# Transposing transfers from SP in place of TensorE's turns of the q and k halves, in a language-model tower block

## The reference

```python
xn = layernorm(layernorm(h)) * norm_g + norm_b
q = heads(xn @ Wq);  k, v = heads(x @ Wkv)           # x = layernorm(h)
k, v = two learned null keys and values, then k, v   # 2050 keys
q = q / |q| * q_scale;  k = k / |k| * k_scale
sim = q @ k.T * 8 - slope(head) * distance           # causal
out = softmax(sim) @ v;  h = h + out @ Wout
```

## Time and profile before

| | |
|---|---|
| median of 3 runs | 2745.8 us (2736.39 to 2750.08) |
| profiled execution | 2751.77 us, span 2750.0 us |
| PE busy | 2424.1 us, 88% |
| DVE busy | 2027.2 us, 74% |
| POOL busy | 1594.1 us, 58% |
| ACT busy | 1406.6 us, 51% |
| mean granted PE clock | 0.948 of full |
| transfers | 106.65 MB, mean 39 GB/s |

### The profile page before, as it was taken

The page is one execution under the profiler, slowest core; times in us unless marked ns, Lnnn a source line. Parts: engine busy times, 40 slices in busy tenths (PEclk is TensorE's granted clock), DMA queues, the critical chain, the costliest instruction groups (busy, mean ns, idle before and its releaser), DMA issues.

```text
span 2750.0 us, 49117 instructions
## 1 busy us (share of the span) xinstructions
PE 2424.1 (88%) x13353; PEld 1204.6 (44%) x13353; DVE 2027.2 (74%) x5748; ACT 1406.6 (51%) x3094; POOL 1594.1 (58%) x1901
## 2 busy tenths in 40 slices
PE   2789999999989988898999999999999997877887
PEld 2434344444434434343444444444434443446775
DVE  6678787878777878878787878787878786644444
ACT  3445455655554646565555555554646563324541
POOL 6365656666675656575757575656565665462424
PEclk8899999999999999999999999999999998868999
DMA  2000111011111011011111000001000002023543
GB/s 46 18 19 19 34 25 37 24 36 26 30 45 23 24 25 31 20 34 28 34 28 30 17 22 15 25 16 25 16 25 15 21 15 82 9 86 112 163 128 123
DMA packets 155702, 106.65 MB, mean 39 GB/s; under 512 B 63728, under 2 KB 139632, under 8 KB 155440
## 3 DMA queue, kind: packets, MB, share of 16 engines
q1 hardware_dynamic: 147760, 82.52, 11.6%
q0 software_dynamic: 7680, 20.98, 2.5%
HBM read 52.94 MB, written 33.29 MB: 31 GB/s over the span
## 4 chain that ended last, share of the span: by engine, by line
PE 29%; DVE 10%; DMA 6%; issue 5%; POOL 2%; SPq 2%; ACT 2%; another core or an unknown queue 1%; ACTq 0%; DVEq 0%; POOLq 0%
PE ps L1474 5%; PE ps L1458 3%; DVE ps L1123 3%; PE ps L1459 3%; DMA rl<-l_row 3%; PE ps L1555 2%; PE ps L1431 2%; PE ps L1541 2%; PE ps L1403 2%; DMA l_row<-l_col 2%; PE ps L1494 1%; PE ps L1400 1%; DVE acc L1161 1%; DVE tqk L1096 1%; PE ps L1484 1%
## 5 line engine op out<-in xcount | busy, mean ns | idle before, releaser
L790 POOL TENSOR_TENSOR acc<-acc,probs 128x512 f32<-128x512 f32 (+4 forms) x944 | 911.5, 966 | 200.3 <-ACT probs L919 114.8
L919 ACT ACTIVATE probs<-ps,btab 128x512 f32<-128x512 f32 (+4 forms) x1408 | 775.5, 589 | 445.8 <-PE ps L1459 282.8
L1123 DVE CUSTOM_DVE_ANT_0 ps<-ps,tab_l 128x512 f32<-128x512 f32 (+1 forms) x896 | 565.9, 671 | 172.4 <-PE ps L1431 170.3
L1474 PE MATMUL ps<-probs,arena 128*64 128x512 f32 (+4 forms) x2816 | 642.7, 534 | 0.0
L1458 PE MATMUL ps<-arena 128*128 128x512 f16 (+4 forms) x1408 | 482.8, 343 | 23.1 <-ACT probs L919 10.6
L1459 PE MATMUL ps<-arena 128*128 128x512 f16 (+9 forms) x1408 | 479.6, 341 | 0.0
L1431 PE MATMUL ps<-arena 64*128 64x512 f16 (+4 forms) x1408 | 247.2, 344 | 120.1 <-DVE mx L1123 115.3
L768 POOL TENSOR_SCALAR nsq<-ssq 128x4 f32<-128x4 f32 (+1 forms) x272 | 62.0, 228 | 475.3 <-DVE ssq L1083 474.2
L771 POOL TENSOR_TENSOR rnorm<-nsq,minus_half 128x4 f32<-128x4 f32 (+1 forms) x272 | 282.6, 1039 | 22.6
L1403 PE MATMUL ps<-wqkv,xT 128*128 128x256 f32 (+1 forms) x1088 | 287.4, 388 | 0.0
L1431 PEld LDWEIGHTS ps<-arena 64*128 64x128 f16 x1408 | 74.9, 93 | 464.1 <-issue 454.4
(11 more groups left out here) (176 smaller groups left out, 3350.5 us busy)
## 6 DMA issues: line engine op xcount, KB each, us to landing
arena<-arena SPq DMA_DIRECT2D x512, 32.0 KB, 1.9
rl<-l_row SPq DMA_DIRECT2D x128, 128.0 KB
x_rows<-arena SPq DMA_DIRECT2D x78, 128.0 KB, 2.2
arena<-x_rows SPq DMA_DIRECT2D x78, 128.0 KB
y_rows<-arena SPq DMA_DIRECT2D x78, 128.0 KB
wqkv<-in_Wkv SPq DMA_DIRECT2D x32, 128.0 KB, 2.4
arena<-in_w SPq DMA_DIRECT2D x2, 2048.0 KB, 11.3
out<-h SPq DMA_DIRECT2D x8, 512.0 KB
```

The source lines that it names most:

```text
L790: pool.tensor_tensor(a, probs[0:rows, (n - 2) % PB, 0:GW] if first else a, p, ALU.add).then_inc(sum_pool, 1)
L919: nc.scalar.activation(probs[0:rows, n % PB, 0:w], bank(S0 + n % 2)[0:rows, 0:w], ACT.Exp, bias=btab[0:rows, hh, z:z + 1]).then_inc(exp_do ...
L1123: nc.vector.tensor_tensor_reduce(bank(A0 + hd)[:, 0:w], bank(A0 + hd)[:, 0:w], tab, 1.0, NEG, ALU.add, ALU.max, mx[:, hd, it, c:c + 1]).th ...
L1474: mm(bank(O0 + o % 2)[DH * hd:DH * hd + DH, c0:GW], vt[t % 2][0:rows, jt, hd, :], probs[0:rows, n % PB, 0:GW - c0], start=(jt == 0), stop= ...
```

## The change

The turns leave PE, and the copies out of PSUM leave ACT. SP waits for `blk` and issues four transposing transfers for each group (128 partitions x 256 fp16 values, 64 KB each; one of 16 partitions for the last group), straight from `blk` into `stk`. `copy_low`, and the scores on PE, wait for those transfers' semaphores. The null keys are copied by ACT in a step of its own, `null_k`, behind the landing of group 0. The turns no longer take a shared PSUM bank or a place of `turn_of`. `stk` grows by 14 columns to a width of 2064. In the plan `copy_low` moves from 0.9 to 3.0 units behind the turn, and `halves` from 3.0 to 5.2.

```diff
-                s1 = turn_of(s0 + lag["turn"])
+                s1 = s0 + lag["turn"]
                 at(s1, "turn", t, g)
-                at(s1 + 0.8, "keep", t, g)
-                at(s1 + 0.8 + 0.1, "copy_low", t, g)
-                halves[(t, g)] = s1 + 3.0
+                if g == 0:
+                    at(s1 + 3.0, "null_k", t)
+                at(s1 + 3.0, "copy_low", t, g)
+                halves[(t, g)] = s1 + 3.0 + 2.2
...
-    SHARED = ("proj", "sums", "turn_shift", "wout", "turn", "turn_x", ...
+    SHARED = ("proj", "sums", "turn_shift", "wout", "turn_x", ...
...
+        NS = N + 16
+        STK, LOW, VT = 2 * NS, 2 * NK, TK * 2 * DH
...
+            def turn(t, g):                                   # SP
+                r = t % 2
+                sp.wait_ge(blk_ready, PG * t + g + 1)
+                need(sp, s_ready, PAIR * (t - 1))
+                if g < PG - 1:
+                    for z in range(2):
+                        for i in range(2):
+                            o, n = 512 * z + 256 * i, 256 * g + 128 * i
+                            sp.dma_start(stk[r][:, z, :, n:n + 128], blk[:, g % 2, o:o + 256], transpose=True).then_inc(turned[g], 16)
+                else:
+                    sp.dma_start(stk[r][:, 1, :, N:NS], blk[0:16, g % 2, 512:768], transpose=True).then_inc(turned[g], 16)
...
             def copy_low(t, g):
-                sp.wait_ge(ta_done, PG * t + g + 1)
+                sp.wait_ge(turned[g], (64 if g < PG - 1 else 16) * (t + 1))
...
             def high(t, g):                                   # ACT
-                need(act, tr_done, PG * t + g - 1)
+                k = PG * t + g - 2 if g >= 2 else PG * t - 1 - g
+                if k >= 0:
+                    act.wait_ge(turned[k % PG], (64 if k % PG < PG - 1 else 16) * (k // PG + 1))
...
-            def keep(t, g):                                   # ACT, all of it
+            def null_k(t):
+                p, r = t % NP, t % 2
+                act.wait_ge(turned[0], 64 * (t + 1))
+                nc.scalar.activation(stk[r][:, 1, :, 0:NN], null_ka..., ACT.Copy).then_inc(nk_in, 1)
...
-            def turn(t, g):                                   # PE, all of it
...
             def scores(t, m):                                 # PE
-                    pe.wait_ge(ta_done, PG * t + min(2 * ig + 3, PG))
+                    for g in range(min(2 * ig + 3, PG)):
+                        pe.wait_ge(turned[g], (64 if g < PG - 1 else 16) * (t + 1))
```

More of the change, by code:

```diff
@@ L309, in lm_tower_kernel @@
     plan.sort()
-    SHARED = ("proj", "sums", "turn_shift", "wout", "turn", "turn_x", "turn_y", "logits", "count", "null_turn")
+    SHARED = ("proj", "sums", "turn_shift", "wout", "turn_x", "turn_y", "logits", "count", "null_turn")
     shared, nth = {}, {}
@@ L373, in lm_tower_kernel @@
         blk = sb("blk", [128, 2, 1152], fp16)
-        STK, LOW, VT = 2 * NK, 2 * NK, TK * 2 * DH
+        NS = N + 16
+        STK, LOW, VT = 2 * NS, 2 * NK, TK * 2 * DH
         arena = [sb(f"arena{i}", [128, STK + LOW + VT]) for i in range(2)]
@@ L484, in lm_tower_kernel @@
         blk_ready = sem("blk_ready")
-        tr_done = sem("tr_done")
-        ta_done = sem("ta_done")
+        turned = [sem(f"turned{i}") for i in range(PG)]
         nk_in = sem("nk_in")
@@ L538, in lm_tower_kernel @@
         NPAR = 8
-        RELEASE = {"proj": p_read, "sums": l_read, "turn_shift": aug_kept, "wout": w_added, "turn": ta_done,
+        RELEASE = {"proj": p_read, "sums": l_read, "turn_shift": aug_kept, "wout": w_added,
                    "turn_x": xt_out, "turn_y": yt_out, "logits": lg_ready, "count": placed, "null_turn": null_ready}
@@ L674, in _ @@
                     spread_l(*which)
+                elif kind == "turn":
+                    turn(*which)
                 elif kind == "copy_low":
@@ L890, in high @@
                                          tqk[0:NN, g % 2, 256:384].rearrange("p (e d) -> p e d", d=DH), ACT.Copy).then_inc(hi_ready, 1)
-            def keep(t, g):
[L893 to L907, removed]
+            def null_k(t):
+                p, r = t % NP, t % 2
+                act.wait_ge(turned[0], 64 * (t + 1))
+                nc.scalar.activation(stk[r][:, 1, :, 0:NN], null_ka[:, 2 * NN * p:2 * NN * (p + 1)].rearrange("p (a n) -> p a n", a=2),
+                                     ACT.Copy).then_inc(nk_in, 1)
             def exp(t, m):
@@ L994, in _ @@
                     high(*which)
-                elif kind == "keep":
-                    keep(*which)
+                elif kind == "null_k":
+                    null_k(*which)
                 elif kind == "tables":
@@ L1404, in proj @@
                 last.then_inc(proj_done, 1)
-            def turn(t, g):
[L1407 to L1420, removed]
             def scores_a(t, n):
@@ L1601, in _ @@
                     proj(*which)
-                elif kind == "turn":
-                    turn(*which)
                 elif kind == "turn_x":
```

## The result

The changed kernel takes 2794.5 us (median of 4 runs, 2784.68 to 2795.75), the kernel before, on the same chip, 2747.9 (4 runs, 2736.39 to 2750.51). The ratio is 1.017, with a 95% interval of 1.0132 to 1.0208: slower by 1.7%, where 1.9% faster was forecast. The time lies in the stated range, and on the second rival's 2794, by luck: that rival's reason, late halves, did not happen, as will be seen. The profiled executions differ less than the medians, 2782.9 against 2750.0 us of span, 32.9 us. What follows accounts for those.

The account below looks back on a forecast made before the run. PE was taken as the bound, 92.8% busy in the steady window. From 2745.8 us, -57 and -5 (PE), -3 (ACT), +10 (SP) and +3 (start) gave 2694; the forecast's own range was 2665 to 2730, the overall range 2665 to 2810.

Parts of the forecast that it names:

- the second rival: Transposing transfers land too late, so PE waits for the halves; at 10.5 us a group, 2794 us; chance 0.19.
- PE's part: Turns holding PE for 85.1 us leave; a third is swallowed by waits for DVE, 57 us pass.
- the first rival: DVE's rhythm: PE waits for DVE's maxima, 75% of the 85 us is swallowed, 2735 us; chance 0.11.
- the prediction's last sentence: Signs of error, among them PE's granted clock falling from 0.98 in the window as its idle share grows; no size given.
- The smaller term of PE's part: PE's wait for `blk` before the turns leaves its queue: 5 us gained, between 0 and 15.
- ACT's part: 128 copies, 129.6 us, leave ACT; shorter PE waits for `exp` gain 3 us, from 0 to 11.
- SP's part: Transposing issues in SP's queue delay the steps of the softmax sums: 10 us lost, from 0 to 20.
- T: Time from the end of `low` until a group's halves stand in `stk`: taken as 6 us, hidden behind the pair before.
- the sums: Steps `turn_l` and `spread_l` queued behind SP's bursts: 1.9 us a pair for DVE's `divide`, 14 us reaching PE.
- The start: First pair: later first score and groups needing transfers plus copies, 3 us lost, from 0 to 20.
- It just fits: In the first pair, a group's 8.4 us on PE must hold 6 us of transfer latency plus 2.4 of four copies.
- The sum: Whole kernel: -57 - 5 - 3 + 10 + 3 = -52 us, giving 2694 from the median.

Follow-up runs that it names:

- e2: The changed kernel with each group's four transposing transfers replaced by one plain transfer, transposition left out, score scale 1e-3: ratio 1.0053 to the kernel before.
- e3: The changed kernel with the turn's place in the plan set by turn_of as before, leaving a hole there: ratio 1.0211 to the kernel before.
- e1: The changed kernel with eight dummy transposes of the identity on PE in the place of every turn: ratio 1.0183 to the kernel before.
- e7: The changed kernel with four dummy matmuls ahead of seven score blocks a pair, where PE waits for DVE: ratio 1.0151 to the kernel before.
- e15: e2 with the dummy matmuls of e7 added: ratio 1.0000 to the kernel before.
- e8: The kernel before with three dummy matmuls ahead of eight score blocks a pair, where PE waits for DVE: ratio 1.0000 to the unmodified kernel before.
- e11: e2 with DVE's row maxima taken over only the last 128 columns of each unit: ratio 0.9600 to the kernel before.
- e13: The changed kernel with one plain transfer a group in the first pair only, transposing ones in the others: ratio 1.0144 to the kernel before.
- e14: The changed kernel with transposing transfers in the first pair only, one plain transfer a group in the others: ratio 1.0128 to the kernel before.
- e4: The kernel before with eight dummy transposes ahead of each group's turns: ratio 1.0089 to the unmodified kernel before.
- e9: The kernel before with DVE's row maxima taken over only the last 128 columns of each unit: ratio 0.9684 to the unmodified kernel before.

## Why the prediction was wrong

**The step that failed is PE's part:** "I let a third be swallowed [...]: 57 us pass." None passes. With the transposing transfers taken out of the account (e2), the ratio is 1.005 (1.0033 to 1.0073), a loss of 14 us. The steady part is 2161.8 us against 2156.4 before, on another chip. The bounds given there, "a quarter of the 85" to "all of it", excluded this. Two things eat the 80 us. PE reaches the maxima earlier and waits longer for DVE, as the first rival said, which put it at three quarters at most. And the granted clock falls, which makes the work that stays take longer; that stood in the prediction's last sentence as a sign of error, without a price, and it is the larger part, some 66 us against 40 in the changed kernel. Shown: the clock's fall (to 0.934 in e2 and 0.928 in e3, from 0.958 on their chip) and its return with dummy work, by half in e1 (0.945 against e3) and in full in e7 and e15 (medians of 0.952 and 0.956, the kernel before's on their chips being 0.953 and 0.956); that dummy work in the waits is free or better (e8, e15); and that with DVE's load taken away the removed work begins to show (e11). Not settled: how the loss divides between the two as causes. Waits and clock move together, and the lower clock makes PE busy for longer, so each part is measured by busy times, not by an experiment that holds the other still; and e7 lifted the clock without a gain that the medians show. That it is the waits for DVE that bring the clock down is argued from where the dummies helped, not shown by itself.

The smaller term of PE's part, 5 us for its wait for `blk` before the turns, is of the right size: in the fifteen pairs that wait was 8.7 us, and 4.3 us of waiting for the transfers' landings stand in its place.

**ACT's part** was right: 117 us left ACT, and PE's wait for `exp` fell from 10.6 to 5.2 us, near the 3 us counted. ACT stood for the landing ahead of `null_k` in 3 pairs of 16, for 3.3 us in all.

**SP's part and T.** T was taken as 6 us and is about 6.2, but made up otherwise: 5.1 us of issuing instead of 2.3, and the last landing 1.2 us behind it. The halves are in time (2.1 us of waiting for them in the fifteen pairs), so the second rival did not happen there, though its time did. The burst on SP was mis-sized by 2.8 us a group: the term was given as 10 us, between 0 and 20, and measured as 21 (the steady windows of e13 and e2; 25 by their ratios). It also went by another path. The prediction priced the sums, yet PE's wait for `divide` fell, from 41.0 to 17.7 us. What stands behind a burst and is waited for is `put_shift`, which the prediction left out of SP's queue; PE's wait for its rows is 5.9 us in e2's steady window, 15.1 in e13's.

**The start** was given as 3 us, between 0 and 20, and is 11.4 in the profiled pair of kernels and 17 between e14 and e2. "It just fits" failed by the same issue time: 6 + 2.4 us a group was counted as T and four copies, but SP itself is held for 5.1 + 2.5 = 7.6 of them with groups waiting behind each other, and the first `put_shift` stands behind them for 8.9 us.

**The sum** as measured in the profiles: +5 (PE's and ACT's work and the new plan, e2) + 20 (SP in the steady pairs) + 11 (start) - 4 (end) = +33 against the forecast -52. The +5 compares two chips and is rough. By the ratios, each against its own chip, the change loses 47 us, of which e2 has 14 (with the start that e2 shortens), and SP and the start the other 32. The forecast's range of 2665 to 2730 was narrower than its terms: their bounds, added up, give 2635 to 2765, and the time lies outside that too.

## What to carry to other kernels

A busy share of 92% does not make an engine the bound. Add work to it before taking work away: 99 us put into PE's waits here cost nothing, and a slope test such as e4 (90 us of work for 23 us of time) would have warned before the change was made. It gives a quarter of the 85 us, 21 us, as what their removal could bring; e2 then lost 14, so the test is a warning and not a price. Where TensorE's granted clock in the profile is already below full and the engine waits often, work taken from it may come back as time at the lower level, as here; with DVE light, where the waits were shorter, a part of it showed (e11). The work to cut here was DVE's: the light maxima of e9 beat both kernels, 0.968 (0.9645 to 0.9723), at the price of a softmax shift taken over fewer keys, whose safety depends on the range of the scores.

## What the runs showed of the hardware

- A transposing transfer of 128 x 256 fp16 (64 KB) from SBUF to SBUF held SP for 1.27 us at issue and landed 2.4 us after it; a plain one of 32 KB held it for 0.58 and landed after 1.9. Eight plain issues cost the kernel as much as four transposing ones (1.022 and 1.017).
- The same kernel before took 2698 to 2748 us on the chips used, 1.8% apart. In the profiles most of that lies behind the last pair's first score, 435 to 453 us on the chips of 2698 and 2712 us and 474 to 483 on those of 2731 and 2748.
- The granted clock of PE went from 0.948 to 0.926 when 3.5% of its work was taken away. With 99 us of dummy matmuls put into its waits it was 0.962 (median of e8's runs), against 0.953 without them on the same chip. The Trainium skill ("TensorE: Matmul & The Clock Gate", The HAM clock gate) says that activity releases the throttle, and the traces agree: at 0.99 in e8's steady part PE is idle for 120 us, at 0.94 in the changed kernel's for 214.
